# Masking the diagonal of causal attention on VectorE instead of GpSimd, in a one-core float32 layer

## The chip, the cores and the metric

One Trainium2 chip, of which the program uses a single core. The metric is the device time of one execution in microseconds (us), median of three runs.

## The reference

Input x is 2 batches of 2048 tokens, 1024 wide, float32. There are 32 query heads of 32 and a single key and value head.

```python
q = (x @ wq_w.T + wq_b).reshape(b, t, H, HD)
k1 = (x @ wk_w.T + wk_b); v1 = (x @ wv_w.T + wv_b)
scores = jnp.einsum('bqhd,bkd->bhqk', q, k1) / jnp.sqrt(jnp.float32(HD))
causal = jnp.tril(jnp.ones((t, t), dtype=bool))
scores = jnp.where(causal, scores, -jnp.inf)
weights = jax.nn.softmax(scores, axis=-1)
attn = jnp.einsum('bhqk,bkd->bqhd', weights, v1).reshape(b, t, H * HD)
x = _layernorm(x + attn @ wo_w.T + wo_b)
x_sim, w_sim = clip(x * x_scale, -448, 448), clip(w * w_scale, -448, 448)
x = _layernorm(x + x_sim @ w_sim * (1.0 / (x_scale * w_scale)))
```

## The kernel before

The program has three stages: the q, k, v projection (to 468 us of the span), attention with the output projection and the first layer norm woven in (to 2254 us), and the last product with the second layer norm. Five queues (TensorE, VectorE, ScalarE, GpSimd and the DMA queue SP) are written out by hand and meet at semaphores. Each engine runs its queue in order, so an instruction that waits holds all behind it.

Attention runs over batches b (2), blocks j of 512 queries (4), and groups of four heads (8 for a block), two groups to a pair: r = 0 and r = 1. A group goes through its key tiles t = 0 to 4j+3, of 128 keys each. The last four, t = 4j to 4j+3, lie on the diagonal: there the first 0, 128, 256 or 384 queries are left out, and the next 128 columns of each head are a square of which one triangle must become zero. Below, step t of a group is:

- TensorE: the scores of step t+1 (L1172), then `weigh_values` of step t-1 (L1184), then in a window of steps a part of the output projection of the block before (L1160). At the last step it takes the scores of the next group's step 0, and then `weigh_values` of the last two steps. At t = 1 come the denominators of the group before (L1194), at t = 3 their spreading (L1202).
- ScalarE: the exponentials of the four heads in two halves (L703), from one set of four PSUM banks into one of four slots of `prob`. It waits until `weigh_values` and the addition of step t-4 have read the slot.
- GpSimd, for diagonal tiles: `affine_select` over 4 x 128 columns in place (L540), which raises `masked`. Its queue also holds, for each pair with j > 0, `att_lo` (L532, which the projection waits for), the addition of bias to the residual tile `res` (L544), and two small instructions of the layer norm (L478, L480).
- VectorE: adds the probabilities over the key tiles into `acc` (L945 for steps 0 and 1 together, L948 after). It waits for `p_done`, on the diagonal also for `masked`. In the same queue: `invert` of the denominators at t = 2 (L909), `normalise_group` at t = 3 (L915), for j = 0 and r = 0 two clippings of a weight piece (L957, L959) at t = 2, and for j > 0 and r = 1 the residual and the layer norm of a tile: `add_residual` (L922), `moments_of` (L767, L769) after the addition of step t = min(2j+6, 4j+3), which is 7, 10 and 12 for j = 1, 2 and 3; then, after the last addition, `normalise` (L774) and `largest` (L926).

`weigh_values` of a diagonal tile waits on TensorE for `masked`:

```python
pe.wait_ge(p_done, s0 * 2 + (2 * t + 4))
if t >= QT * j:
    pe.wait_ge(masked, n * QT + (t - QT * j + 1))
for h in range(HG):
    last = nc.tensor.matmul(bank[h * HD:(h + 1) * HD, 4 + r, off:NB], v_sb[:, t], prob[:, t % SLOTS, h, off:NB], ...)
```

Of the kernel before, what the change touches and what calls it, by code (L numbers as in the profile page):

```python
# [31 lines left out]
ALU = mybir.AluOpType  # L32
# [4 lines left out]
P = 128  # L37
# [4 lines left out]
MASKED = -3.0e38  # L42


def build(nc, x_t, x, w_qkv, b_qkv, w_o, b_o, w_f, out, B, T, H):
# [5 lines left out]
    JB = T // NB  # L51
# [35 lines left out]
    with ctx:  # L87
        def sb(name, shape, dt=F32, stack=ctx):
            return stack.enter_context(nc.sbuf_tensor(name, shape, dt))
# [7 lines left out]
        small = sb("small", [P, 32])  # L97
        exponent = sb("exponent", [P, 1])
        flag = sb("flag", [P, 1], I32)

        with ExitStack() as s:
            w_hi = sb("w_hi", [P, MT, KT, P], F32R, s)
# [124 lines left out]
        s_done = sem("s_done")  # L227
        p_done = sem("p_done")
        masked = sem("masked")
        pv_done = sem("pv_done")  # L230
        acc_done = sem("acc_done")
        den_done = sem("den_done")
# [223 lines left out]
        def _(pool):  # L456
# [15 lines left out]
            pool.wait_ge(consts, 7 + HG)  # L472
            nc.gpsimd.tensor_copy(ident_bf[:], ident[:]).then_inc(consts, 1)

            def inverse_deviation(moments, done, before):

                wait_apart(pool, done, before + (NH + 1))
                nc.gpsimd.tensor_scalar(moments[:, 1:2], moments[:, 1:2], LN_EPS, None, ALU.add).then_inc(done, 1)  # L478
                wait_apart(pool, done, before + (NH + 2))
                nc.gpsimd.tensor_tensor(moments[:, 2:3], moments[:, 1:2], exponent[:], ALU.pow).then_inc(done, 1)  # L480
# [45 lines left out]
            with pool.Fori(0, B) as b:  # L526
                def body(j, gp, first, last):
                    if j > 0:
                        tile = projected(b, j, gp)
                        wait_apart(pool, att_hi_cut, tile + 1)  # L530
                        heads = att[:, (j - 1) % 2 * G:(j - 1) % 2 * G + G, bass.ds(gp * P, P)]
                        nc.gpsimd.tensor_tensor(att_lo[:], heads, att_hi[:].bitcast(F32), ALU.subtract).then_inc(att_cut, 1)  # L532
                    for r in range(2):
                        n, s0 = group(b, j, gp, r), step(b, j, gp, r)
                        for i in range(QT):
                            t = QT * j + i
                            off = first_query(j, t)
                            wait_apart(pool, p_done, s0 * 2 + (2 * t + 4))
                            tri = prob[:, t % SLOTS, :, off:off + P]
                            nc.gpsimd.affine_select(out=tri, in_=tri, compare_op=ALU.is_ge, fill=0.0, base=0,  # L540
                                                    pattern=[[0, HG], [1, P]], channel_multiplier=-1).then_inc(masked, 1)
                        if j > 0 and r == 0:
                            pool.wait_ge(res_in, stored_alone(b, j, gp) * 16 + 16)
                            nc.gpsimd.tensor_tensor(res[:], res[:], bo[:], ALU.add).then_inc(res_ready, 1)  # L544
                    if j > 0:
                        inverse_deviation(moments[:, 0], ln1, tile * LN + LN)

                pairs_of_groups(pool, b, body)
                for t in range(QT):
                    tile = projected(b, JB, t)  # L550
                    pool.wait_ge(att_hi_cut, tile + 1)
                    heads = att[:, (JB - 1) % 2 * G:(JB - 1) % 2 * G + G, t * P:(t + 1) * P]
                    nc.gpsimd.tensor_tensor(end_lo[:, t % 2], heads, end_hi[:, t % 2].bitcast(F32), ALU.subtract).then_inc(att_cut, 1)
                    pool.wait_ge(end_in[t], b * 16 + 16)
                    nc.gpsimd.tensor_tensor(end_res[:, t], end_res[:, t], bo[:], ALU.add).then_inc(res_ready, 1)
                    if t >= 1:
                        inverse_deviation(moments[:, (t - 1) % 2], ln1, (tile - 1) * LN + LN)
                inverse_deviation(moments[:, (QT - 1) % 2], ln1, projected(b, JB, QT - 1) * LN + LN)
# [204 lines left out]
        def _(dve):  # L763
# [119 lines left out]
            dve.wait_ge(wo_cut, KT)  # L883


            dve.wait_ge(flag_ready, 1)
            needed = dve.value_load(flag[0:1, 0:1], min_val=0, max_val=1)
            with dve.If(needed == 1):
# [39 lines left out]
            with dve.Fori(0, B) as b:  # L928
                def body(j, gp, first, last):
                    for r in range(2):  # L930
                        n, s0 = group(b, j, gp, r), step(b, j, gp, r)
                        NT = key_tiles(j)
                        dve.wait_ge(den_done, n + 1)
                        for t in range(NT):
                            off = first_query(j, t)
                            if t >= 1:
                                dve.wait_ge(p_done, s0 * 2 + (2 * t + 4))
                                if t >= QT * j:
                                    dve.wait_ge(masked, n * QT + (t - QT * j + 1))
                                new = prob[:, t % SLOTS, :, off:NB]  # L940
                                if t == 1:
                                    if off > 0:
                                        nc.vector.tensor_copy(acc[:, r, :, 0:off], prob[:, 0, :, 0:off])

                                    nc.vector.tensor_tensor(acc[:, r, :, off:NB], prob[:, 0, :, off:NB], new, ALU.add).then_inc(acc_done, 2)  # L945
                                else:
                                    dve.wait_ge(acc_done, s0 + (t + SLOTS))
                                    nc.vector.tensor_tensor(acc[:, r, :, off:NB], acc[:, r, :, off:NB], new, ALU.add).then_inc(acc_done, 1)  # L948

                            if t == 2 and not (first and r == 0):  # L950
                                invert(n - 1)
                            if t == 3 and not (first and r == 0):
                                normalise_group(n - 1, group_before(j, gp, r))
                            if j == 0 and r == 0 and t == 2:
                                piece = b * (G // 2) + gp
                                dve.wait_ge(piece_in, piece * 16 + 16)
                                nc.vector.tensor_scalar(wf_piece[:], wf_piece[:], small[:, 15:16], FP8_MAX, ALU.mult, ALU.min).then_inc(piece_clip, 1)  # L957
                                dve.wait_ge(piece_clip, piece * 2 + 1)
                                nc.vector.tensor_scalar(wf_piece[:], wf_piece[:], -FP8_MAX, None, ALU.max).then_inc(piece_clip, 1)  # L959
                            if j > 0:  # L960
                                tile = projected(b, j, gp)
                                if r == 1 and t == 1:
                                    add_residual(res[:], tile, 0, Y_BANK)
                                if r == 1 and t == min(NT // 2 + 4, NT - 1):
                                    add_residual(res[:], tile, 1, Y_BANK)
                                    dve.wait_ge(y_read, tile * 2 + 4)
                                    moments_of(res[:], stats[:, 0], moments[:, 0], ln1, tile * LN + LN)
                                if r == 1 and t == NT - 1:
                                    normalise(res[:], moments[:, 0], ln1, tile * LN + LN)
                                    largest(res[:], tile)  # L970

                pairs_of_groups(dve, b, body)
                invert(b * SEQ_GROUPS + (SEQ_GROUPS - 1))
                normalise_group(b * SEQ_GROUPS + (SEQ_GROUPS - 1), att[:, (JB - 1) % 2 * G + G - 1])

                def end_normalise(t):
                    tile = projected(b, JB, t)
                    normalise(end_res[:, t], moments[:, t % 2], ln1, tile * LN + LN)
                    largest(end_res[:, t], tile)

                for t in range(QT):
                    tile = projected(b, JB, t)
                    for half in range(2):
                        add_residual(end_res[:, t], tile, half, Y_BANK - half)
                    dve.wait_ge(y_read, tile * 2 + 4)
                    if t >= 1:
                        end_normalise(t - 1)
                    moments_of(end_res[:, t], stats[:, t % 2], moments[:, t % 2], ln1, tile * LN + LN)
                end_normalise(QT - 1)
# [334 lines left out]
```

## Time and profile before

| | |
|---|---|
| median of 3 runs | 2735.11 us (2733.13 to 2735.16) |
| the profiled execution | 2732.4 us, span 2730.7 us |
| granted TensorE clock, mean | 0.971 of full |
| busy: TensorE, VectorE, ScalarE, GpSimd | 93%, 69%, 47%, 32% |
| the chain that ended last | TensorE 77%, issue 7%, VectorE 5%, ScalarE 4%, GpSimd 3%, DMA 3% |
| `affine_select` of GpSimd | 256, 300.4 us busy |
| additions of VectorE into `acc`, L948 | 512, 1093.1 us busy |

The span runs from the first to the last instruction; the time also holds what lies around it (1.7 us). Busy shares are over the whole span, though attention, the longest stage, is where the changed instructions are.

### The profile page before, as it was taken

The page shows a single profiled execution, that of the slowest core. Times are in us where ns is not written, and L with a number is a line of the kernel's source. Part 1 is how long each engine was busy: PE and PEld are TensorE (multiplying, and loading weights), DVE is VectorE, ACT ScalarE, POOL GpSimd, SP SyncE. Part 2 cuts the span into 40 slices and gives each one's busy share as a digit, 9 for nine tenths or more (in the row PEclk, how much of TensorE's full clock was granted, in tenths as well). Part 3 has the DMA queues.
Part 4 walks back from the last instruction along what each step waited for, and adds up shares of the span by engine and source line. Part 5 has one row for each costly group of instructions (what it writes and reads, how often), then busy time and mean ns, then how long its engine had stood idle before and what let it go on. Part 6 is the DMA issues. An engine that isn't in the chain of part 4 may idle for free.

```text
span 2730.7 us, 45644 instructions
## 1 busy us (share of the span) xinstructions
PE 2538.9 (93%) x15400; PEld 1587.0 (58%) x15400; DVE 1876.7 (69%) x1432; ACT 1274.1 (47%) x1571; POOL 865.2 (32%) x572
## 2 busy tenths in 40 slices
PE   7999996889999999999888999999999997699998
PEld 5888884545544444444554555444444446588887
DVE  6343335657888889999555778888899993444444
ACT  2222213555566667777335555666677670100000
POOL 2321302424322222122333334222212213466663
PEclk9999997999999999999988999999999998799999
DMA  7343325512111110110333112111101004122221
GB/s 237 118 146 139 115 108 170 137 40 70 39 48 50 47 39 20 31 39 28 86 89 100 51 58 55 44 39 39 39 28 39 29 11 154 49 90 85 92 92 62
DMA packets 78776, 201.47 MB, mean 74 GB/s; under 512 B 8672, under 2 KB 10720, under 8 KB 76512
## 3 DMA queue, kind: packets, MB, share of 16 engines
q1 hardware_dynamic: 51360, 140.01, 17.8%
q10 hardware_dynamic: 27328, 60.30, 5.8%
q8 instruction: 53, 0.87, 0.1%
q14 instruction: 35, 0.29, 0.0%
HBM read 125.83 MB, written 74.45 MB: 73 GB/s over the span
## 4 chain that ended last, share of the span: by engine, by line
PE 77%; issue 7%; DVE 5%; ACT 4%; POOL 3%; DMA 3%; ACTq 1%; SPq 1%; DVEq 0%; POOLq 0%
PE bank L1172 16%; PE bank L1184 15%; PE bank L1083 14%; PE bank L1160 14%; PE bank L1269 13%; ACT prob L703 4%; PE bank L1202 2%; DVE acc L948 2%; DMA q_st<-max_d 2%; PE bank L1194 2%; POOL prob L540 1%; PE bank L1258 1%; DVE acc L945 1%; PE bank L1069 1%; DMA xt_raw<-x_t 1%
## 5 line engine op out<-in xcount | busy, mean ns | idle before, releaser
L703 ACT ACTIVATE prob<-bank 128x1024 f32<-128x1024 f32 (+3 forms) x1280 | 1077.6, 897 | 622.4 <-PE bank L1172 589.7
L948 DVE TENSOR_TENSOR acc<-acc,prob 128x2048 f32<-128x2048 f32 (+3 forms) x512 | 1093.1, 2135 | 130.2 <-POOL prob L540 84.9
L1172 PE MATMUL bank<-q_st,k_st 98*128 98x512 f32 (+3 forms) x2560 | 709.9, 391 | 104.3 <-ACT prob L703 62.5
L1172 PEld LDWEIGHTS bank<-q_st,k_st 98*128 98x128 f32 x2560 | 425.8, 191 | 407.0 <-ACT prob L703 310.0
L1184 PE MATMUL bank<-prob,v_sb 128*32 128x512 f32 (+3 forms) x5120 | 595.9, 547 | 11.0 <-POOL prob L540 10.8
L540 POOL TENSOR_SCALAR_AFFINE_SELECT prob<-prob 128x512 f32<-128x512 f32 x256 | 300.4, 1177 | 882.8 <-ACT prob L703 882.2
L1083 PE MATMUL bank<-xt_hi,w_hi 128*128 128x512 f32 x576 | 228.4, 397 | 16.3 <-DVE xt_lo L790 15.6
L1083 PE MATMUL bank<-xt_hi,w_lo 128*128 128x512 f32 x576 | 227.4, 395 | 0.0
L1083 PE MATMUL bank<-xt_lo,w_hi 128*128 128x512 f32 x576 | 227.3, 395 | 0.0
L1184 PEld LDWEIGHTS bank<-prob,v_sb 128*32 128x32 f32 x5120 | 107.7, 109 | 197.0 <-issue 139.2
L1269 PE MATMUL bank<-wf_hi,xs_hi 128*128 128x512 f32 x512 | 202.5, 396 | 0.0
L1269 PE MATMUL bank<-wf_lo,xs_hi 128*128 128x512 f32 x512 | 199.9, 390 | 0.0
L1269 PE MATMUL bank<-wf_hi,xs_lo 128*128 128x512 f32 x512 | 199.9, 390 | 0.0
L743 ACT ACTIVATE xs_hi<-bank 128x1024 fp32r<-128x1024 f32 x32 | 32.9, 1027 | 343.8 <-DVE y L774 328.2
L624 ACT ACTIVATE raw<-bank,bias 128x512 f32<-128x512 f32 x64 | 44.0, 687 | 296.7 <-PE bank L1083 284.5
L945 DVE TENSOR_TENSOR acc<-prob 128x2048 f32<-128x2048 f32 (+1 forms) x64 | 137.8, 2153 | 60.2 <-ACT prob L703 60.2
L809 DVE CAST part_hi<-raw 128x512 fp32r<-128x512 f32 x64 | 41.2, 643 | 199.9 <-ACT raw L624 180.3
L532 POOL TENSOR_TENSOR att_lo<-att,att_hi 128x1024 fp32r<-128x1024 f32 x24 | 64.6, 2693 | 321.5 <-ACT att_hi L713 298.1
L1160 PE MATMUL bank<-wo_hi,att_hi 128*128 128x512 f32 x384 | 166.0, 432 | 0.0
L1160 PE MATMUL bank<-wo_hi,att_lo 128*128 128x512 f32 x384 | 158.4, 413 | 0.0
L1160 PE MATMUL bank<-wo_lo,att_hi 128*128 128x512 f32 x384 | 157.7, 411 | 0.0
L1160 PEld LDWEIGHTS bank<-wo_hi,att_hi 128*128 128x128 f32 x384 | 72.2, 188 | 124.2 <-issue 115.4
(118 smaller groups left out, 2664.9 us busy)
## 6 DMA issues: line engine op xcount, KB each, us to landing
q_st<-q_hi_d SPq DMA_DIRECT2D x128, 256.0 KB
xt_raw<-x_t SPq DMA_DIRECT2D x16, 1024.0 KB, 7.0
q_hi_d<-part_hi ACTq DMA_DIRECT2D x64, 256.0 KB, 2.1
q_lo_d<-part_lo ACTq DMA_DIRECT2D x64, 256.0 KB, 2.3
q_st<-q_lo_d SPq DMA_DIRECT2D x64, 256.0 KB
x<-x_d SPq DMA_DIRECT2D x32, 512.0 KB, 3.2
out<-y ACTq DMA_DIRECT2D x32, 512.0 KB, 2.6
res<-x SPq DMA_DIRECT2D x24, 512.0 KB, 3.4
```

Of the source, the lines that this page charges most:

```text
L532: nc.gpsimd.tensor_tensor(att_lo[:], heads, att_hi[:].bitcast(F32), ALU.subtract).then_inc(att_cut, 1)
L540: nc.gpsimd.affine_select(out=tri, in_=tri, compare_op=ALU.is_ge, fill=0.0, base=0, pattern=[[0, HG], [1, P]], channel_multiplier=-1).then ...
L703: nc.scalar.activation(prob[:, t % SLOTS, 2 * p:2 * p + 2, off:NB], bank[:, 2 * p:2 * p + 2, off:NB], ACT.Exp, scale=SCALE).then_inc(p_don ...
L945: nc.vector.tensor_tensor(acc[:, r, :, off:NB], prob[:, 0, :, off:NB], new, ALU.add).then_inc(acc_done, 2)
L948: nc.vector.tensor_tensor(acc[:, r, :, off:NB], acc[:, r, :, off:NB], new, ALU.add).then_inc(acc_done, 1)
L1083: last = nc.tensor.matmul(dst, (w_hi, w_lo)[a][:, m, k], (xt_hi[:, r], xt_lo[r])[c][:, k], start=(k == 0 and a == c == 0), stop=(k == KT - ...
L1160: last = nc.tensor.matmul(bank[:, y_bank], (hi, lo)[a][:, k], (wo_hi, wo_lo)[c][:, k, cols], start=(i == 0), stop=(i == len(todo) - 1), sk ...
L1172: last = nc.tensor.matmul(bank[:, h, off:NB], k_st[:, t * P:(t + 1) * P], q_st[:, slot, h, off:NB], start=True, stop=True)
L1184: last = nc.tensor.matmul(bank[h * HD:(h + 1) * HD, 4 + r, off:NB], v_sb[:, t], prob[:, t % SLOTS, h, off:NB], start=(t == 0), stop=(t == ...
L1194: last = nc.tensor.matmul(bank[c * HD:(c + 1) * HD, DEN_BANK, 0:P], head_col[:, h], acc[:, r, h, c * P:(c + 1) * P], start=(h == 0), stop= ...
L1202: last = nc.tensor.matmul(bank[:, DEN_BANK, c * P:(c + 1) * P], spread[:, c], r_den[:], start=True, stop=True)
L1269: last = nc.tensor.matmul(bank[:, 4 + 2 * (r % 2) + h], (xs_hi, xs_lo)[a][:, r % 2, k], (wf_hi, wf_lo)[c][:, k, cols], start=(k == 0 and a ...
```

## The change

A constant tile `limit` (128 x 128) is built once on GpSimd: a very large number where the key may be seen, zero elsewhere. On each diagonal tile VectorE takes the minimum of the square of the four heads with `limit`, repeated over the heads, and raises `masked`. It does so in its own queue, just ahead of the addition of the same step. GpSimd has no `affine_select` in attention any more, and no body for the block j = 0. TensorE's and ScalarE's queues are as they were. VectorE now also waits for `p_done` at step 0.

```diff
+            nc.gpsimd.memset(limit[:], -MASKED).then_inc(limits, 1)
+            pool.wait_ge(limits, 1)
+            nc.gpsimd.affine_select(out=limit[:], in_=limit[:], compare_op=ALU.is_ge, fill=0.0, base=0,
+                                    pattern=[[0, 1], [1, P]], channel_multiplier=-1).then_inc(limits, 1)
...
                     for r in range(2):
-                        n, s0 = group(b, j, gp, r), step(b, j, gp, r)
-                        for i in range(QT):
-                            t = QT * j + i
-                            off = first_query(j, t)
-                            wait_apart(pool, p_done, s0 * 2 + (2 * t + 4))
-                            tri = prob[:, t % SLOTS, :, off:off + P]
-                            nc.gpsimd.affine_select(out=tri, in_=tri, compare_op=ALU.is_ge, fill=0.0, base=0,
-                                                    pattern=[[0, HG], [1, P]], channel_multiplier=-1).then_inc(masked, 1)
                         if j > 0 and r == 0:
                             pool.wait_ge(res_in, stored_alone(b, j, gp) * 16 + 16)
                             nc.gpsimd.tensor_tensor(res[:], res[:], bo[:], ALU.add).then_inc(res_ready, 1)
...
-                pairs_of_groups(pool, b, body)
+                for j in range(1, JB):
+                    with pool.Fori(0, G // 2) as gp:
+                        body(j, gp, False, False)
...
                         for t in range(NT):
                             off = first_query(j, t)
+                            dve.wait_ge(p_done, s0 * 2 + (2 * t + 4))
+                            if t >= QT * j:
+                                own = prob[:, t % SLOTS, :, off:off + P]
+                                nc.vector.tensor_tensor(own, own, limit[:].to_broadcast([P, HG, P]), ALU.min).then_inc(masked, 1)
                             if t >= 1:
-                                dve.wait_ge(p_done, s0 * 2 + (2 * t + 4))
                                 if t >= QT * j:
                                     dve.wait_ge(masked, n * QT + (t - QT * j + 1))
                                 new = prob[:, t % SLOTS, :, off:NB]
```

The first place is VectorE's queue in block j = 3, group r = 1, from the addition of step 12 to that of step 13. Before (L948 is the addition, L922, L767 and L769 are the residual and the moments):

```order
L948 TENSOR_TENSOR acc<-acc,prob 128x2048
L920 REGISTER_ALU
L922 TENSOR_TENSOR res<-bank,res 128x512
L966 REGISTER_ALU
L767 BN_STATS stats<-res 128x6 x2
L317 ISA
L769 BN_AGGR moments<-stats 128x2
L937 REGISTER_ALU
L939 REGISTER_ALU
L947 REGISTER_ALU
L948 TENSOR_TENSOR acc<-acc,prob 128x4x384
```

The same place in the changed kernel, where the lines have moved by one to five (L953 is the addition, L941 the minimum):

```order
L953 TENSOR_TENSOR acc<-acc,prob 128x2048
L922 REGISTER_ALU
L924 TENSOR_TENSOR res<-bank,res 128x512
L971 REGISTER_ALU
L768 BN_STATS stats<-res 128x6 x2
L319 ISA
L770 BN_AGGR moments<-stats 128x2
L938 REGISTER_ALU
L941 TENSOR_TENSOR prob<-prob,limit 128x4x128
L944 REGISTER_ALU
L952 REGISTER_ALU
L953 TENSOR_TENSOR acc<-acc,prob 128x4x384
```

The mask of step 13, which stood in GpSimd's queue, now stands behind the addition of step 12 and behind the residual and the moments.

The second place is GpSimd's queue in a pair of groups with j = 3, from `att_lo` to the bias addition. Before:

```order
L532 TENSOR_TENSOR att_lo<-att,att_hi 128x1024
L317 REGISTER_ALU
L540 AFFINE_SELECT prob<-prob 128x4x128
L317 REGISTER_ALU
L540 AFFINE_SELECT prob<-prob 128x4x128
L317 REGISTER_ALU
L540 AFFINE_SELECT prob<-prob 128x4x128
L317 REGISTER_ALU
L540 AFFINE_SELECT prob<-prob 128x4x128
L543 ISA
L544 TENSOR_TENSOR res<-res,bo 128x1024
```

The same place in the changed kernel, with the layer norm's two small instructions that follow it:

```order
L539 TENSOR_TENSOR att_lo<-att,att_hi 128x1024
L542 ISA
L543 TENSOR_TENSOR res<-res,bo 128x1024
L319 ISA
L485 TENSOR_SCALAR moments<-moments 128x1
L319 REGISTER_ALU
L487 TENSOR_TENSOR moments<-moments,exponent 128x1
```

The bias addition now stands directly behind `att_lo`, ahead of the diagonal, where four masks stood between them.

## Rows read from the trace of the kernel before

**Rows 1.** The page: each engine's busy time, share and instructions.
```profile
PE 2538.9 (93%) x15400; PEld 1587.0 (58%) x15400; DVE 1876.7 (69%) x1432; ACT 1274.1 (47%) x1571; POOL 865.2 (32%) x572
```

**Rows 2.** Busy time by stretch, first batch: j = 0, 1, 2, 3.
```profile
core 0: us, PE busy (x) PEld busy (x) DVE busy (x) ACT busy (x) POOL busy (x), PEclk, DMA share, GB/s
469.60:547.70 78.10, 66.23 (x642) 38.31 (x641) 47.89 (x53) 44.54 (x72) 37.18 (x32) 0.92 0.54 136
547.70:748.60 200.90, 184.14 (x1289) 103.30 (x1288) 144.96 (x96) 110.13 (x141) 65.68 (x46) 0.97 0.19 51
748.60:1004.50 255.90, 248.62 (x1666) 126.39 (x1664) 225.58 (x132) 171.69 (x205) 64.39 (x48) 1.00 0.15 42
1004.50:1328.00 323.50, 316.43 (x2046) 152.17 (x2048) 295.90 (x165) 233.68 (x268) 70.61 (x47) 1.00 0.11 31
```

**Rows 3.** VectorE by line and shape: count, busy us, mean ns, idle before.
```profile
L948 DVE TENSOR_TENSOR acc<-acc,prob 128x2048 f32<-128x2048 f32 x336 | 820.2, 2441 | 79.3 <-POOL prob L540 46.8 <-ACT prob L703 27.6
```

**Rows 4.** The masks' own line (min/median/max ns), and TensorE's waits for them.
```profile
L540 POOL TENSOR_SCALAR_AFFINE_SELECT prob<-prob x256: 625/1111/2732, 471.7 to 2254.6; 128x512 f32<-128x512 f32 x128
...
PE bank L1184 <- POOL prob L540: 10.8, 7, 4.3
```

**Rows 5.** Timeline, diagonal of one group j = 3, r = 1: start us, us.
```profile
1242.95 2.29 DVE L948 TENSOR_TENSOR acc<-acc,prob 128x2048 f32<-128x2048 f32 x1 [1.33 <-POOL prob L540]
1245.16 0.68 DVE L922 TENSOR_TENSOR res<-bank,res 128x512 f32<-128x512 f32 x1
...
1247.32 0.21 DVE L769 BATCH_NORM_AGGREGATE moments<-stats 128x2 f32<-128x12 f32 x1 [0.15 <-DVE stats L767]
1247.60 3.75 DVE L948 TENSOR_TENSOR acc<-acc,prob 128x1536 f32<-128x1536 f32 x3
...
1246.36 0.85 PE L1184 MATMUL bank<-prob,v_sb 128*32 128x384 f32 x8
1248.27 0.86 PE L1184 MATMUL bank<-prob,v_sb 128*32 128x256 f32 x16
```

**Rows 6.** Timeline, one group j = 3, r = 0, then one of j = 2, r = 0.
```profile
1185.01 15.99 DVE L948 TENSOR_TENSOR acc<-acc,prob 128x2048 f32<-128x2048 f32 x6
1187.00 2.53 POOL L532 TENSOR_TENSOR att_lo<-att,att_hi 128x1024 fp32r<-128x1024 f32 x1 [17.06 <-ACT att_hi L713]
1202.20 1.06 PE L1184 MATMUL bank<-prob,v_sb 128*32 128x512 f32 x8
...
890.09 14.33 DVE L948 TENSOR_TENSOR acc<-acc,prob 128x2048 f32<-128x2048 f32 x5
902.35 1.06 PE L1184 MATMUL bank<-prob,v_sb 128*32 128x512 f32 x8
```

**Rows 7.** Timeline, end of one group j = 2, r = 1.
```profile
940.80 0.86 PE L1184 MATMUL bank<-prob,v_sb 128*32 128x256 f32 x16
...
942.05 0.21 DVE L769 BATCH_NORM_AGGREGATE moments<-stats 128x2 f32<-128x12 f32 x1 [0.15 <-DVE stats L767]
```

**Rows 8.** Timeline, one group j = 1, r = 0, and the first one of all (last row).
```profile
664.75 4.34 DVE L948 TENSOR_TENSOR acc<-acc,prob 128x2048 f32<-128x2048 f32 x1
674.90 3.35 POOL L544 TENSOR_TENSOR res<-res,bo 128x1024 f32<-128x1024 f32 x1
669.65 1.07 PE L1184 MATMUL bank<-prob,v_sb 128*32 128x512 f32 x8 [1.04 <-POOL prob L540]
...
573.01 1.93 PE L1184 MATMUL bank<-prob,v_sb 128*32 128x512 f32 x8 [4.29 <-POOL prob L540]
```

**Rows 9.** Timeline, one group j = 0, r = 0.
```profile
493.34 1.75 DVE L945 TENSOR_TENSOR acc<-prob 128x1536 f32<-128x1536 f32 x1
496.85 0.95 DVE L909 RECIPROCAL r_den<-bank 128x128 f32<-128x128 f32 x1
...
498.41 0.69 DVE L959 TENSOR_SCALAR wf_piece<-wf_piece 128x1024 f32<-128x1024 f32 x1
...
497.02 0.89 PE L1184 MATMUL bank<-prob,v_sb 128*32 128x256 f32 x16
```

More of the change, by code:

```diff
@@ L99, in build @@
         flag = sb("flag", [P, 1], I32)
+        limit = sb("limit", [P, 1, P])
         with ExitStack() as s:
@@ L229, in build @@
         masked = sem("masked")
+        limits = sem("limits")
         pv_done = sem("pv_done")
@@ L883, in _ @@
             dve.wait_ge(wo_cut, KT)
+            dve.wait_ge(limits, 2)
             dve.wait_ge(flag_ready, 1)
```

## The prediction, made before the changed kernel had run

> **What bounds the kernel now.** I read the page first: TensorE is busy 93% of the span and VectorE 69% [rows 1], so the question is whether VectorE has room where the change puts work. That the whole span cannot say, so I split it by stretches. In j = 2 TensorE is busy 248.6 of 255.9 us and in j = 3 316.4 of 323.5: TensorE sets the time there, and whatever holds its queue is added to the end. VectorE has 30.3 and 27.6 us free in these two, 3.8 and 3.5 us for each of eight groups [rows 2]. The second batch repeats the first.
>
> The views of the masks say that they cost TensorE little today: it waited 10.8 us for them in all, in 7 places, although a mask takes 1111 ns in the middle [rows 4]. The reason is in the order: `weigh_values` of step t stands behind the scores of step t+1 and a piece of projection, so GpSimd, with nothing else to do, has a step's time to answer. The median is far above the shortest, 625 ns, because GpSimd and VectorE hold each other up: an addition that takes 2.29 us alone [rows 5] took 4.34 us when `att_lo` had begun before it [rows 8], which is 2.29 plus what was left of `att_lo`. The additions of 2048 columns have a mean of 2441 ns [rows 3].
>
> So the reader should look at VectorE's queue on the diagonal. A mask will be ready only when VectorE reaches it, and VectorE is often behind: additions of 2.29 us follow each other without a pause through j = 3, r = 0 [rows 6].
>
> **The price of one minimum.** The trace has no minimum with a repeated operand. The nearest row is the VectorE instruction on 512 float32 columns with two tensor inputs, 0.68 us [rows 5]; the last addition of the row of three is of that shape too: 3.75 less 1.75 [rows 9] less about 1.23 for 1024 columns leaves 0.7. I take 0.69 and 0.07 to the next start, m = 0.76 us. From below, half of a clipping of 1024 columns (0.69 us [rows 9]) would be 0.35; from above, the mask's own median of 1.11 [rows 4].
>
> The Trainium skill, "VectorE: DVE Perf Modes", section on the TRN2 errata, has a formula for a float32 `tensor_tensor` of N columns, (N+151)/0.96 ns; for 512 that is 691 ns, an estimate for an operation that no row here shows.
>
> 256 minima at 0.76 are 195 us of VectorE, 3.0 us for each group, against 3.5 us free in j = 3. What counts is not this sum but how late each mask is. I walk through each kind of group with the present times, moving only what the change moves.
>
> **j = 3, r = 1** [rows 5]. Step 12 is masked in time. Its addition ends at 1245.2, then residual and moments until 1247.53; only then can the minimum of step 13 run, 1247.55 to 1248.25. TensorE wants it at 1246.36: 1.9 us late. TensorE goes on (0.8 us of values, 1.0 of scores) and wants step 14 at 1250.2. VectorE: addition 13 (1.75) to 1250.05, minimum to 1250.8: 0.65 late. Then addition 14 (1.23), minimum 15 at 1252.8; TensorE wants it at 1251.3: 1.5 late. Together 4.1 us.
>
> **j = 3, r = 0** [rows 6]. Here six additions run without a pause to 1201.0, `att_lo` having held one of them. Two things move. The bias addition on GpSimd, 3.35 us now with its waiting [rows 8], of which I take 2.4 as its own work (`att_lo`, of the same size, took 2.53), stood behind the four masks; now it follows `att_lo` at once and blocks the next VectorE addition for 2.4 us, ahead of the diagonal. And VectorE starts the group 1.6 us earlier against TensorE, since TensorE lost 4.1 us in the group before and VectorE's own chain only 2.5 (three minima and the turn to the first of them). So addition 11 ends at 1201.8 and the minimum of step 12 at 1202.5; TensorE wants it at 1202.20: 0.35 late. By the same steps as above, with projection pieces of 1.0 us between, step 13 is 0.55 late, step 14 in time, step 15 1.5 late. Together 2.4 us.
>
> **j = 2.** r = 1: the residual stands after step 10, so one minimum is behind it. The moments end at 942.26, which becomes 942.7 with the minima of steps 8 to 10 and without the waits for GpSimd; minimum 11 is done at 943.45. TensorE wants it 0.43 us behind 940.80, about 941.25 [rows 7]: 2.2 late. r = 0: five additions run to 904.42 [rows 6], the last being that of step 8, and TensorE wants the mask of step 8 at 902.35. Its minimum comes before that addition, behind addition 7 (to 901.8); with 2.4 us for the bias addition and 0.7 gained as above it ends at 903.8, 1.4 late; step 11 is 0.7 late. Together 2.1 us.
>
> **j = 1.** r = 1: the residual comes after all minima, and they are in time: 0. r = 0: the addition locked by `att_lo` ends at 669.09 [rows 8]; then the waiting bias addition takes its turn, to 671.5, and minimum 4 is done at 672.2. TensorE's values started at 669.65, after a wait of 1.04 for the mask: 2.5 us later than now. The first such group of all is different: TensorE waited 4.29 us there [rows 8], because GpSimd came to j = 1 late and had `att_lo` and masks to do; that wait goes.
>
> **j = 0.** VectorE does everything for one group in some 9 us. Minima 0 and 1 fit in idle time; then the addition to 495.2 [rows 9], minimum 2, addition 2, `invert` to 498.2, for r = 0 the clippings (0.65 and 0.69) to 499.7, and only then minimum 3: done at 499.0 (r = 1) or 500.4 (r = 0). TensorE wants it at 497.48, the second half of the last row: 1.5 or 2.95 late. The spacing of groups, now 8.74 us at its shortest, becomes 10.95 on average; it is 78.1/8 = 9.76 now [rows 2], since other groups wait for queries by DMA, which the longer group hides. 1.2 us each.
>
> **The sum.** j = 0: 16 x 1.2 = 19. j = 1: 7 x 2.5 - 4.3 = 13. j = 2: 8 x (2.2 + 2.1) = 34. j = 3: 8 x (4.1 + 2.4) = 52, less 4, since in the last group of either batch no scores follow and VectorE's own chain, later by some 2.2 us, counts. Together 114; less 0.2 us in each of 24 groups where TensorE today waits for ScalarE after the turn to a new group: 109. On the profiled execution's own 2732.4 us that is 2841. The median lies 2.7 us above that execution, within what separates the runs, so I say 2842, slower by 3.9%. Building the constant costs nothing: GpSimd does it ahead of the attention, where it waits for TensorE; if it did not, it would be under 1 us. The wait for `p_done` at step 0 holds nothing, since step 1's addition waits for a later one. The GpSimd masks that go give back VectorE's locked time (part of 2441 less 2291 ns, some 25 us over all additions), which is in the walks above.
>
> Of the unknown prices: about 135 minima stand on TensorE's path in these walks (3 in each group of j = 0, 1 in r = 0 of j = 1, 4 in a pair of j = 2, 6 in a pair of j = 3). With m = 0.42 the sum is 63, with 1.18 it is 166. If the bias addition never blocks, it is 34 less, 75: 1.65 in seven groups of j = 1, about 1.4 in sixteen of j = 2 and 3.
>
> On this blocking the rows speak first: 4.34 against 2.29. The Trainium skill, "SBUF — State Buffer", section "Who interferes with whom", says that a VectorE instruction with two SBUF inputs and a GpSimd instruction that reads SBUF exclude each other for a whole instruction, whoever issues first going ahead. By that the minimum takes part in the exclusion too, and `att_lo` or the bias addition can stand in front of a mask; without it the sum would be the 75 of the sentence above. I keep 109.
>
> **Rivals.**
> - *The masks come in time and the kernel is faster* (8%). VectorE needs 0.69 us where GpSimd needs 1.11, and has 3.5 us free a group. If its lag at the diagonal were under the step of TensorE that lies between exponential and `weigh_values`, nothing would wait, and TensorE would win its 10.8 us: 2724. It decides at j = 3, r = 1: with residual and moments between two masks (2.3 us) the lag is over a step. Against it stands that place alone already. The Trainium skill, "GPSIMD Engine Reference", section "Engine selection", sends elementwise work on a tile to VectorE and calls GpSimd about twice as slow for two inputs; taken alone it points to this rival.
> - *The lags are half made up* (14%): the bias addition doesn't collide, and VectorE's relief from locked additions brings it in step in r = 0. Then only j = 0 and r = 1 of j = 2 and 3 are left: 19 - 4 + 8 x 2.2 + 8 x 4.1 - 4 = 61, so 2796.
> - *VectorE becomes the bound, or the clock falls* (12%). In j = 3 VectorE has 0.5 us left a group at the present pace; if small GpSimd work (`moments`) locks out minima between the residual and the end, each pair of j = 2 and 3 loses 2 to 3 us more, 16 x 2.5 = 40, so 2882. In j = 0 the granted clock is 0.92 already [rows 2]; longer pauses could keep more of it at the lower level (1.2 GHz), and some 20 us more.
> - *It changes nothing* (5%): gains and losses cancel, 2735.
>
> **How the numbers follow.** The forecast has 61%: 2810 to 2870 by its own prices. The range must leave out 20% at most: from 2780, which takes in most of the second rival, to 2885. What is left out is the 8 and 5% below and some of the third above. A difference of 0.2% is about what can be told from none here. Faster 7%, same 5%, slower 88%.
>
> **What the profile after would show.** The minimum at 0.69 us; additions of 2048 columns nearer 2291; TensorE waiting in `weigh_values` for VectorE's minimum, about 4 us in j = 3, r = 1, split 1.9, 0.65, 1.5, and 2.2 at the last step of j = 2, r = 1; almost none in j = 1, r = 1; the bias addition right behind `att_lo` with a blocked addition or minimum beside it; groups of j = 0 near 11 us; stretches of 88, 204, 273 and 346 us for j = 0 to 3. If the minimum takes another time, or VectorE arrives at the diagonal without lag, the prediction is wrong.

## The result, and the profile after

The changed kernel takes 2868.47 us (median of 4 runs, 2865.95 to 2868.93) against 2734.4 (the kernel before, now also a median of 4): a ratio of 1.049 (95% interval 1.047 to 1.051). It is slower by 134 us; 107 were forecast, in a range from 2780 to 2885. The profiled execution has a span of 2864.2 us, 133.5 more than before, at a mean granted clock of 0.953.

The page of the changed kernel, busy times and then the chain that ended last:

```profile
PE 2592.2 (91%) x15400; PEld 1602.8 (56%) x15400; DVE 2011.4 (70%) x1688; ACT 1274.4 (44%) x1571; POOL 610.9 (21%) x318
...
PE 62%; DVE 15%; issue 14%; ACT 4%; DMA 2%; POOL 1%; ACTq 1%; DVEq 1%; SPq 0%; POOLq 0%
```

VectorE now holds 15% of the chain, where it held 5. But TensorE's busy time has grown too, by 53 us with the same 15400 matmuls [rows 1]; the prediction's walks had nothing of that kind. The stretches of the first batch, j = 0, 1, 2, 3, answer to [rows 2]:

```profile
core 0: us, PE busy (x) PEld busy (x) DVE busy (x) ACT busy (x) POOL busy (x), PEclk, DMA share, GB/s
467.00:548.90 81.90, 67.85 (x641) 39.15 (x641) 65.06 (x82) 44.52 (x72) 0.00 (x0) 0.91 0.51 130
548.90:759.50 210.60, 187.99 (x1289) 105.81 (x1288) 166.20 (x132) 110.17 (x140) 28.22 (x14) 0.96 0.18 48
759.50:1036.40 276.90, 256.54 (x1666) 128.84 (x1665) 240.48 (x163) 171.81 (x205) 39.25 (x16) 0.97 0.14 39
1036.40:1389.30 352.90, 328.67 (x2034) 155.51 (x2032) 310.87 (x193) 233.16 (x266) 43.43 (x16) 0.96 0.10 28
```

They are longer by 3.8, 9.7, 21.0 and 29.4 us, together 63.9 of the half that falls to one batch. TensorE's busy time in them is larger by 1.6, 3.9, 7.9 and 12.2, together 25.6, and its clock is 0.97 and 0.96 in j = 2 and 3, where it was 1.00. So two things must be told apart: waits, and a slower clock behind them.

VectorE by line and shape (count, busy us, mean ns), and TensorE's waits in the whole span (us, times, longest), which answer to [rows 3] and [rows 4]:

```profile
L941 DVE TENSOR_TENSOR prob<-prob,limit 128x512 f32<-128x512 f32 x256 | 187.1, 731 | 41.6 <-ACT prob L704 41.6
L953 DVE TENSOR_TENSOR acc<-acc,prob 128x2048 f32<-128x2048 f32 x336 | 848.2, 2524 | 55.4 <-ACT prob L704 44.6
...
PE bank L1189 <- DVE prob L941: 107.6, 94, 3.3
PE bank L1165 <- POOL att_lo L539: 3.1, 1, 3.1
```

TensorE waits 107.6 us for masks, in 94 places, where it waited 10.8. Its wait for queries by DMA went the other way, first before and then in the changed kernel:

```profile
PE bank L1172 <- DMA q_st<-max_d: 36.8, 8, 24.8
PE bank L1177 <- DMA q_st<-max_d: 25.6, 2, 25.2
```

The account nearly closes: 96.8 us more of waits for masks, 53.3 more of busy time, 3.1 for `att_lo`, less 11.2 for queries and 6.1 for VectorE's additions (6.6 us before, 0.5 now) come to 136, where the span grew by 133.5. The long additions of VectorE have not become faster without the masks of GpSimd: 2524 ns instead of 2441.

The diagonal of one group j = 3, r = 1 in the changed kernel (start us, us), the place of [rows 5]:

```profile
1213.56 0.21 DVE L770 BATCH_NORM_AGGREGATE moments<-stats 128x2 f32<-128x12 f32 x1 [0.15 <-DVE stats L768]
1213.68 0.68 DVE L941 TENSOR_TENSOR prob<-prob,limit 128x512 f32<-128x512 f32 x1
1216.16 0.68 DVE L941 TENSOR_TENSOR prob<-prob,limit 128x512 f32<-128x512 f32 x1
1218.11 0.68 DVE L941 TENSOR_TENSOR prob<-prob,limit 128x512 f32<-128x512 f32 x1
...
1214.41 0.85 PE L1189 MATMUL bank<-prob,v_sb 128*32 128x384 f32 x8 [1.67 <-DVE prob L941]
1215.20 1.72 PE L1177 MATMUL bank<-q_st,k_st 98*128 98x512 f32 x4
1216.90 1.08 PE L1189 MATMUL bank<-prob,v_sb 128*32 128x256 f32 x8
1218.85 0.65 PE L1189 MATMUL bank<-prob,v_sb 128*32 128x128 f32 x8 [0.87 <-DVE prob L941]
1219.43 2.08 PE L1177 MATMUL bank<-q_st,k_st 98*128 98x512 f32 x4
```

The reader sees both effects. The minimum of step 13 starts when the moments are done, and TensorE's values follow 0.05 us behind it after a wait of 1.67 us. Then four scores take 1.72 and 2.08 us that took 1.09 just before, at 1205.73 us: TensorE runs at 1.2 GHz there. The granted clock, in the order of the columns above, before the wait and after it:

```profile
1204.00:1208.00 4.00, 4.00 (x25) 1.75 (x25) 3.42 (x2) 3.13 (x4) 0.00 (x0) 1.00 0.00 0
1218.00:1224.00 6.00, 4.89 (x20) 2.53 (x24) 4.70 (x6) 3.35 (x6) 0.00 (x0) 0.50 0.22 87
```

Since it is slow, it asks for the mask of step 14 only when it is there.

A group j = 3, r = 0, the place of the first part of [rows 6], and then the wait for the first mask of a group j = 1, r = 0, the place of [rows 8]:

```profile
1240.31 4.27 POOL L539 TENSOR_TENSOR att_lo<-att,att_hi 128x1024 fp32r<-128x1024 f32 x1 [23.64 <-ACT att_hi L714]
1244.53 4.43 POOL L543 TENSOR_TENSOR res<-res,bo 128x1024 f32<-128x1024 f32 x1
1237.71 18.06 DVE L953 TENSOR_TENSOR acc<-acc,prob 128x2048 f32<-128x2048 f32 x6
1256.43 1.07 PE L1189 MATMUL bank<-prob,v_sb 128*32 128x512 f32 x8 [0.83 <-DVE prob L941]
1259.45 0.85 PE L1189 MATMUL bank<-prob,v_sb 128*32 128x384 f32 x8 [0.43 <-DVE prob L941]
1263.88 0.42 PE L1189 MATMUL bank<-prob,v_sb 128*32 128x128 f32 x8 [1.19 <-DVE prob L941]
...
670.24 4.40 POOL L543 TENSOR_TENSOR res<-res,bo 128x1024 f32<-128x1024 f32 x1
672.96 2.23 DVE L941 TENSOR_TENSOR prob<-prob,limit 128x512 f32<-128x512 f32 x1
675.24 1.07 PE L1189 MATMUL bank<-prob,v_sb 128*32 128x512 f32 x8 [3.30 <-DVE prob L941]
```

The bias addition stands right behind `att_lo`, and six additions of VectorE take 18.06 us where they took 15.99 [rows 6]. In j = 1 it stops a minimum itself, which takes 2.23 us in place of 0.68, and TensorE waits 3.30 us.

The ends of one group j = 2, r = 1, of a group j = 0, r = 0 and of one j = 0, r = 1, which answer to [rows 7] and [rows 9]:

```profile
899.20 0.43 PE L1189 MATMUL bank<-prob,v_sb 128*32 128x128 f32 x8 [1.61 <-DVE prob L941]
520.26 0.43 PE L1189 MATMUL bank<-prob,v_sb 128*32 128x128 f32 x8 [2.13 <-DVE prob L941]
529.93 0.42 PE L1189 MATMUL bank<-prob,v_sb 128*32 128x128 f32 x8 [0.77 <-DVE prob L941]
```

### The profile page after: what moved, and what is told of

Same layout as the page of the kernel before. It is cut to its first block, busy times and chain, and to the rows that moved or that the text cites. A ratio compares the mean times of both kernels' runs of the same rounds, so it can differ in the third digit from the quotient of the medians.

```text
span 2864.2 us, 45192 instructions
## 1 busy us (share of the span) xinstructions
PE 2592.2 (91%) x15400; PEld 1602.8 (56%) x15400; DVE 2011.4 (70%) x1688; ACT 1274.4 (44%) x1571; POOL 610.9 (21%) x318
## 4 chain that ended last, share of the span: by engine, by line
PE 62%; DVE 15%; issue 14%; ACT 4%; DMA 2%; POOL 1%; ACTq 1%; DVEq 1%; SPq 0%; POOLq 0%
PE bank L1088 13%; PE bank L1274 12%; PE bank L1177 11%; PE bank L1189 11%; PE bank L1165 10%; DVE acc L953 8%; DVE prob L941 4%; ACT prob L704 4%; PE bank L1207 2%; PE bank L1199 2%; PE bank L1263 1%; DVE stats L768 1%; DMA xt_raw<-x_t 0%; PE bank L1074 0%; DVE r_den L911 0%
## 5 line engine op out<-in xcount | busy, mean ns | idle before, releaser
L953 DVE TENSOR_TENSOR acc<-acc,prob 128x2048 f32<-128x2048 f32 (+3 forms) x512 | 1057.3, 2065 | 77.1 <-ACT prob L704 44.6
L1177 PE MATMUL bank<-q_st,k_st 98*128 98x512 f32 (+3 forms) x2560 | 724.6, 400 | 93.1 <-ACT prob L704 63.1
L1189 PE MATMUL bank<-prob,v_sb 128*32 128x512 f32 (+3 forms) x5120 | 622.9, 562 | 107.6 <-DVE prob L941 107.6
L1177 PEld LDWEIGHTS bank<-q_st,k_st 98*128 98x128 f32 x2560 | 438.3, 196 | 397.8 <-ACT prob L704 301.7
L485 POOL TENSOR_SCALAR moments<-moments 128x1 f32<-128x1 f32 x64 | 18.3, 286 | 1284.0 <-DVE moments L770 1284.0
L941 DVE TENSOR_TENSOR prob<-prob,limit 128x512 f32<-128x512 f32 x256 | 187.1, 731 | 41.6 <-ACT prob L704 41.6
L539 POOL TENSOR_TENSOR att_lo<-att,att_hi 128x1024 fp32r<-128x1024 f32 x24 | 87.7, 3655 | 567.7 <-ACT att_hi L714 447.5
```

What stands on the lines that cost most here:

```text
L941: nc.vector.tensor_tensor(own, own, limit[:].to_broadcast([P, HG, P]), ALU.min).then_inc(masked, 1)
L1177: last = nc.tensor.matmul(bank[:, h, off:NB], k_st[:, t * P:(t + 1) * P], q_st[:, slot, h, off:NB], start=True, stop=True)
```

## The experiments

Three theories. **A**: what costs is where a mask stands in VectorE's queue. **B**: what costs is VectorE's added load, wherever it stands. **C**: part of the loss is the clock. Ratios are to the kernel before, with 95% intervals.

**The load alone.** The kernel before, with minima on a scratch tile:

```diff
+                            if t >= QT * j:
+                                nc.vector.tensor_tensor(scratch[:], scratch[:], limit[:].to_broadcast([P, HG, P]), ALU.min).then_inc(spare, 1)
+                                dve.wait_ge(spare, n * QT + (t - QT * j + 1))
```

> The kernel before, with 256 minima of the same shape on a scratch tile in the places where the changed kernel masks; GpSimd masks as before and nobody but VectorE waits for the minima. Theory A (what costs is the mask's place in VectorE's queue): TensorE doesn't wait for the minima, so the time stays near before, 2735 to 2750 us. Theory B (what costs is VectorE's added load of 187 us): 2840 us or more.

2796.26 us, 1.022 (1.021 to 1.024): between the two theories. VectorE's minima and TensorE's waits in this run:

```profile
L945 DVE TENSOR_TENSOR scratch<-scratch,limit 128x512 f32<-128x512 f32 x256 | 251.0, 980 | 34.3 <-ACT prob L709 32.9
...
PE bank L1212 <- DVE r_den L916: 43.0, 34, 2.2
PE bank L1194 <- POOL prob L546: 10.1, 7, 5.5
```

Nobody but VectorE waits for these minima, and still the kernel loses 61 us. TensorE waits for the inverted denominators (43.0 us, where it was 2.9), and is busy 16.5 us more with the same matmuls. Their inversion stands in VectorE's queue at step 2 of the next group: VectorE carries its lateness into the next group. In this run minima and GpSimd's masks also stop each other, so that a minimum takes 980 ns in place of 731; 61 us is therefore likely more than the load alone costs in the changed kernel, but no run tells the two apart. Theory A falls as the only cause, and so does B.

**The moments last.** The changed kernel with

```diff
-                                if r == 1 and t == min(NT // 2 + 4, NT - 1):
+                                if r == 1 and t == NT - 1:
```

> The changed kernel with the second residual half and the moments after the last addition of the group in j = 2 and 3 instead of between two masks. Theory A: the late steps of r = 1 (1.6 us in j = 2; 1.7 and 0.4 to 0.9 in j = 3, 8 groups each) go, some 30 us, VectorE enters r = 0 less far ahead, 5 to 10 us back, and part of the clock's falls goes with the waits: 2815 to 2845 us. Theory B: the same instructions, so 2868 us.

2850.61 us, 1.043 (1.041 to 1.044): 18 us won, short of the expected. TensorE's waits for masks fall from 107.6 to 87.6 us, but it now waits 24.1 for the inverted denominators: what VectorE has not done at the end of one group it owes in the next.

**The bias late.**

```diff
                         if j > 0 and r == 0:
+                            wait_apart(pool, masked, group(b, j, gp, r) * QT + QT)
                             pool.wait_ge(res_in, stored_alone(b, j, gp) * 16 + 16)
```

> The changed kernel, where GpSimd waits for the four masks of r = 0 before it adds the bias, which puts the addition back to its place of before. If the bias addition's lock is what makes the first mask of r = 0 late (3.3 us in j = 1, 1.1 in j = 2, 0.8 in j = 3), 25 to 40 us are won with the clock: 2830 to 2845 us. If the addition is hidden wherever it stands, 2868 us.

2828.94 us, 1.035 (1.034 to 1.037): 40 us won, the upper end of the expected 25 to 40. TensorE's waits and VectorE's long additions, in the profiled execution, which took 2817.58:

```profile
PE bank L1190 <- DVE prob L942: 68.3, 55, 2.1
L954 DVE TENSOR_TENSOR acc<-acc,prob 128x2048 f32<-128x2048 f32 x336 | 811.1, 2414 | 56.2 <-ACT prob L705 45.4
```

The waits for masks are 39 us less than in the changed kernel, and the longest is 2.1. The additions take 2414 ns instead of 2524, which is also less than the 2441 before the change. This is the largest single part that one line takes back, and it is a thing that the change moved without touching it: GpSimd's bias addition slid forward when the masks in front of it went.

**Both.**

> The changed kernel with both the moments behind the last addition and the bias addition behind the masks of r = 0. Theory A: the two places are apart, so their gains of 18 and 40 us add up: 2805 to 2820 us. If VectorE's load is what stays (theory B), removing waits at the masks only moves them to the denominators, which TensorE reads from VectorE two steps later, and less than the sum is won: 2825 us or more.

2804.72 us, 1.027 (1.025 to 1.028). The two gains add up, 64 us against 18 and 40. Yet waits for the inverted denominators stay (22.6 us), beside 53.0 for masks.

**The minima twice, and on half the heads.** The same `tensor_tensor` a second time, or with `0:HG // 2` in place of all heads, which leaves two of the four heads unmasked.

> The changed kernel with each minimum done twice. The prediction's walks have some 135 minima on TensorE's path: 135 x 0.76 = 103 us on top of 2868, 2950 to 2990 us with the clock. If only the load counts beyond what VectorE has free, all 256 would show, 195 us: 3060 us.

> The changed kernel with each minimum on two of the four heads only (0.42 us in place of 0.69; the other two heads keep what the mask would take away). The walks of the prediction put some 135 minima on TensorE's path: 135 x 0.27 = 36 us less, and 10 to 15 for the clock: 2815 to 2835 us. If above a certain load every further minimum counts in full (doubling them cost 203 us, more than their own 195) and below it hardly any, this is on the steep part still and wins 256 x 0.27 = 69 us: 2800 us.

Twice: 3071.3 us, 1.124 (1.122 to 1.125), 203 us above the changed kernel. Half: 2813.38, 1.029 (1.028 to 1.031), 55 us below it. Busy times and TensorE's wait for masks with the minima twice, then the same wait with half of them and the half minimum:

```profile
PE 2685.4 (87%) x15400; PEld 1653.8 (54%) x15400; DVE 2185.0 (71%) x1944; ACT 1274.9 (42%) x1571; POOL 600.9 (20%) x318
PE bank L1192 <- DVE prob L944: 215.9, 113, 4.3
...
PE bank L1189 <- DVE prob L941: 69.6, 83, 3.0
L941 DVE TENSOR_TENSOR prob<-prob,limit 128x256 f32<-128x256 f32 x256 | 116.8, 456 | 53.8 <-ACT prob L704 53.8
```

It is 275 ns shorter; 55 us over 256 minima is 215 ns each, so nearly four fifths of a minimum's time reaches the end. Part of it is the clock: TensorE's busy time falls by 19 us (2592.2 to 2572.8), and its waits for masks by 38, close to the 36 of the walks (135 x 0.27).

Upwards the time lies near the second number, 3060 us, by which all 256 minima count. But the trace does not show VectorE as the bound: it is busy 71% of the span, and from 1100 to 1400 us, in j = 3, 256.5 us of 300. TensorE's waits for masks grow by 108 us, where the walks have 103, and its busy time by 93 with the same matmuls, at a mean clock of 0.915; 11 more are waits for the denominators. So the walks hold for the waits both ways, and what goes beyond them is for the most part TensorE's busy time at the lower clock.

**One step ahead.** With the bias late, and

```diff
-                            if t >= QT * j:
-                                own = prob[:, t % SLOTS, :, off:off + P]
+                            for m in ([0] if t == 0 else [1, 2] if t == 1 else [t + 1] if t + 1 < NT else []) if j == 0 else [m for m in ((t, t + 1) if t == QT * j else (t + 1,)) if QT * j <= t and m < NT]:
+                                at = first_query(j, m)
+                                own = prob[:, m % SLOTS, :, at:at + P]
+                                if m > t:
+                                    dve.wait_ge(p_done, s0 * 2 + (2 * m + 4))
```

> The changed kernel with the bias addition late, and on the diagonal each minimum one step ahead: VectorE masks step t+1 before it adds step t (the first diagonal step stays where it was for j > 0). The same instructions in another order. Theory A: TensorE's waits for masks (68 us in the run with the bias late alone) nearly vanish, and what stays is the wait for the inverted denominators as in the run with idle minima: 2765 to 2795 us. Theory B: 2829 us as with the bias late alone.

2811.74 us, 1.029 (1.028 to 1.031): 17 us better than the bias late alone, less than A expected. TensorE's waits in this run:

```profile
PE bank L1193 <- DVE prob L945: 39.9, 22, 3.0
PE bank L1211 <- DVE r_den L912: 25.5, 16, 2.1
```

Masks cost 28 us less than with the bias late alone, the denominators 23 more (2.1 there) and the queries by DMA 13 more (38.7 us for 25.4). The waits together are not shorter; what is won appears in TensorE's busy time, 22 us less (2583.9 to 2562.3).

**The inversion at step 1**, added to this run and to the one with both:

```diff
-                            if t == 2 and not (first and r == 0):
+                            if t == 1 and not (first and r == 0):
                                 invert(n - 1)
```

> The run with the minima one step ahead, and besides the inversion of the denominators at step 1 instead of step 2, ahead of one addition. TensorE's waits for it (25.5 us there) go if what it suffers from is the place of the inversion in VectorE's queue: 2780 to 2795 us against 2812. If VectorE's total load decides, the wait moves on to the masks of r = 0: 2805 us or more.

> The changed kernel with the bias late, the moments last and the inversion at step 1. TensorE waited 22.6 us for the inversion in the run with the first two: 2780 to 2790 us against 2805 if its place is the cause, 2800 us or more if VectorE's load is.

2803.03 us, 1.026 (1.024 to 1.028), and 2799.91, 1.024 (1.022 to 1.026): 9 and 5 us won of waits of 25.5 and 22.6. The 9 are barely clear of the spread; the 5 are not (2795 to 2809 us, against 2801 to 2807 with both). In the first of the two the waits are now

```profile
PE bank L1193 <- DVE prob L945: 56.3, 42, 3.0
```

The wait for the denominators is down to 2 us, and the one for masks has grown from 39.9 to 56.3: most of it has moved, as B said. The best median of the orders tried is 2799.91 us, still 65 above the kernel before.

**Filler for the clock.** The changed kernel with matmuls that nobody reads ahead of six late masks:

```diff
+                        fillers = {(3, 1, 13): 6, (3, 1, 15): 3, (3, 0, 15): 4, (3, 0, 12): 2, (2, 0, 8): 4, (2, 1, 11): 6}.get((j, r, t), 0)
+                        if fillers:
+                            pe.wait_ge(att_ready, n + 2)
+                        for _ in range(fillers):
+                            nc.tensor.matmul(bank[:, DEN_BANK], wo_hi[:, 0, 0:P], wo_hi[:, 0, 0:512], start=True, stop=True)
                         pe.wait_ge(masked, n * QT + (t - QT * j + 1))
```

> The changed kernel with 2 to 6 matmuls that nobody reads, put in TensorE's queue ahead of the six late masks of j = 2 and 3 (0.22 us each, no more than the wait there). Theory C (part of the loss is TensorE's clock falling to 1.2 GHz after the waits): the busy time of TensorE's own matmuls falls by some 30 us, few stretches of low clock are left, and the time falls to 2830 to 2850 us. If the clock costs nothing beyond the waits: 2868 to 2875 us.

2851.61 us, 1.043 (1.042 to 1.045): 17 us faster with 200 more matmuls, the mean clock 0.967 in place of 0.953. The stretch of j = 3 in the first batch, in the order of the columns of the stretches above:

```profile
1033.50:1384.00 350.50, 335.40 (x2097) 162.44 (x2097) 311.51 (x195) 233.52 (x268) 43.42 (x16) 0.99 0.11 28
```

The clock is 0.99 there instead of 0.96. So C is right in kind, and at least 17 of the 134 us are the clock. It is more if the fillers cost anything themselves, or for the waits in j = 0 and 1, which have none; how much more stays open. An estimate: 200 fillers at 0.22 us each, as above, are 44 of the 2614.8 us that TensorE is busy in this run, which leaves 2571 for the others, 21 less than in the changed kernel.

**The mask ahead of `att_lo`, in the kernel before**, for j = 1, r = 0: an attempt at a version faster than both.

> The kernel before, GpSimd masking as before, but in j = 1, r = 0 the first mask ahead of att_lo. TensorE's wait for that mask (1.04 us in seven groups, 4.29 in the first, 10.8 in all) goes; att_lo comes a mask later, up to 0.5 us late for the projection: 2725 to 2733 us against 2735. If the wait only moves to att_lo: 2735 us.

2732.55 us, 1.000 (0.999 to 1.001). The wait for the mask has become one for `att_lo`, of nearly the same size:

```profile
PE bank L1166 <- POOL att_lo L531: 9.1, 7, 4.3
```

No version tried beats the kernel before.

## Why the prediction was right

**What bounds, and the mechanism**: right. TensorE sets the time in j = 2 and 3, and the minimum in VectorE's queue arrives late. The minimum at 0.69 us (0.68 in the rows above, where nothing stops it) was right, and the places were: 1.67 and 0.87 us at steps 13 and 15 of j = 3, r = 1 (1.9 and 1.5 forecast), 1.61 at the last step of j = 2, r = 1 (2.2), nothing in j = 1, r = 1, and in j = 3, r = 0 0.83, 0.43, none and 1.19 (0.35, 0.55, none and 1.5). At step 14 of r = 1 the forecast 0.65 is missing in the rows shown, because TensorE, slowed, asks later; in the run with filler, where it is not slowed, the wait at this place is 0.50 us:

```profile
1209.89 0.64 PE L1194 MATMUL bank<-prob,v_sb 128*32 128x256 f32 x8 [0.50 <-DVE prob L941]
```

In j = 2, r = 0 the first mask is 1.1 us late (1.4 forecast). The working there does not come out: 901.8 and 2.4, less 0.7, and the minimum make 904.2 and not 903.8.

**The bias addition**: right as a mechanism, and it decides much: 40 us with the clock, 39 of waits for masks, where the prediction had 34 for its blocking. In j = 1, r = 0 TensorE waits 3.30 us where it waited 1.04; 2.5 more were forecast.

**j = 0**: over-sized. 1.2 us a group was the term; the stretch grew by 3.8 in eight groups, 0.5 each. The waits are there, 2.13 and 0.77 us (2.95 and 1.5 forecast), but the longer group hides more than was reckoned: before, TensorE waited 12 us in seven of these groups, 0.7 to 2.2 each, for queries by DMA at the turn to the next group, and in the changed kernel it waits there once, 0.4.

**The first group of j = 1**: wrong. The 4.3 us were to go because GpSimd would come to the block earlier. TensorE no longer waits for the mask, but 3.1 us for `att_lo` itself, so only 1.2 of the 4.3 went. GpSimd starts `att_lo` there at 572.37, with no mask to do before it; why so late, the runs leave open.

**VectorE's relief from locks**: wrong. Additions of 2048 columns were to come nearer 2291 ns; they went to 2524. `att_lo` now collides with VectorE more: its mean rose from 2693 to 3655 ns, and that of the bias addition from 3272 to 4222. What lengthened VectorE's additions was the bias addition's new place: with the bias late it takes 2739 ns and they take 2414, while `att_lo` stays at 3667. So with the masks gone they are shorter than before, by 27 ns, and the slide took more than that away.

**The clock**: left out of the sum, and given only as part of a rival, for j = 0. It is the term that the sum put at nothing: TensorE is busy 53 us more with the same matmuls. Against that the walks' own terms are too high: in the first batch, stretches longer by 63.9 us less 25.6 of busy time leave 38 us of other loss, 77 in two, where the walks had 109. That the time lies only 27 us from the forecast is therefore in part luck: a sum some 30 us too high stands against the clock, up to 53, that was left out.

**The third rival**, VectorE as the bound or the clock falling: the first half did not come about. VectorE is busy 310.9 of 352.9 us in j = 3, 88% where it was 91%, and 85% of the time from 1100 to 1400 us, in j = 3 too, with twice the minima. The clock did fall, but in j = 2 and 3, where the rival had it in j = 0.

**A wait that was missed**: late VectorE costs TensorE at the denominators too. It shows hardly at all in the changed kernel (2.1 us), probably since TensorE's waits at the masks let VectorE catch up, and it is one reason why repairs of the order give back less than the masks' waits.

## What to carry to other kernels

An operation moved from an idle engine to one that is nearly full costs through its place in the queue: ask, for each instance, what stands ahead of it there and when the consumer asks, not only how much idle time the engine has on average. The load counts too: with nobody waiting for the minima the kernel still lost 61 us, at the next thing that TensorE reads from VectorE. Look also at what slides forward on the engine that is relieved; here that was 40 of 134 us, and one wait took it back. And where short waits are added on TensorE, its clock is another price beside the waits; none of the orders tried paid back VectorE's lateness, which moved in part from masks to denominators.

## What the runs showed of the hardware

A wait of 1.67 us was followed by a stretch at 1.2 GHz: the granted clock was 1.00 from 1204 to 1208 us, ahead of the wait, and 0.50 from 1218 to 1224, and matmul groups of four took 2.08 us that took 1.09 ahead of it. With filler in the waits of j = 2 and 3 the clock of j = 3 was 0.99 instead of 0.96.

GpSimd and VectorE stop each other for whole instructions: a minimum took 2.23 us behind a bias addition, 0.68 otherwise. The Trainium skill says the same in "SBUF — State Buffer", section "Who interferes with whom", for a VectorE instruction with two SBUF inputs beside a GpSimd instruction that reads SBUF; the trace agrees, in these numbers and in the addition of 4.34 us [rows 8].
